# An adaLN-conditioned MoE FFN on one core: condition matrices by one gather and a round trip through DRAM, input loads queued ahead, TensorE started on zeros

## The reference, cut to what matters

```python
# x (32, 64, 512), itok (32,) in 1..198, cond weights (200, 64, 64); E=8 experts, H=512, I=352
w   = weights[itok]                                   # one 64x64 matrix for each batch entry
x1  = einsum('bct,bcd->bdt', x, w)                    # conditioned tokens, N = 2048 rows of 512
logits = einsum('nh,eh->ne', x1, Wr); gate = softmax(logits)
top2_val, top2_idx = top_k(gate, 2)                   # capacity 640 rows an expert, rank by cumsum
y   = sum over the chosen experts of gate * (silu(x1 @ Wg.T) * (x1 @ Wu.T)) @ Wd.T
out = x + y
```

## Time and profile before

| | |
|---|---|
| median of 3 runs | 308.54 us (308.44 to 308.93) |
| profiled execution, first to last instruction | 318.2 us |
| start of the expert phase's first transposes in it | 67.25 us |
| PE busy from 75 to 300 us | 224.93 of 225 us |
| mean granted TensorE clock | 0.963 |

### The profile page before, as it was taken

How to read it: one execution, slowest core, us unless ns; L and a number is a source line. 1 busy time by engine, 2 the same in 40 slices (tenths; PEclk the granted TensorE clock), 3 DMA queues, 4 the chain that set the end, 5 groups by cost and what they waited for, 6 DMA issues and landing times.

```text
span 318.2 us, 4646 instructions
## 1 busy us (share of the span) xinstructions
PE 286.5 (90%) x1620; PEld 250.0 (79%) x1621; DVE 134.1 (42%) x259; ACT 125.5 (39%) x212; POOL 138.2 (43%) x128
## 2 busy tenths in 40 slices
PE   2944989898999999999999999999999999999940
PEld 2623645568989999999999999999999999999930
DVE  2305689533434443454345444434544444523200
ACT  2102247612444444543435354445435444523220
POOL 5772007840045443374533334753735456463130
PEclk9985999789999999999999999999999999999995
DMA  6846119399979487866866866979679686474422
GB/s 157 277 157 216 63 47 384 129 319 345 407 188 204 103 226 131 181 174 165 169 141 140 157 121 150 230 157 211 178 168 179 145 195 95 71 116 59 59 35 33
DMA packets 24991, 53.16 MB, mean 167 GB/s; under 512 B 3344, under 2 KB 3344, under 8 KB 24976
## 3 DMA queue, kind: packets, MB, share of 16 engines
q0 software_dynamic: 9472, 21.67, 36.5%
q1 hardware_dynamic: 15504, 31.29, 30.2%
HBM read 32.69 MB, written 20.25 MB: 166 GB/s over the span
## 4 chain that ended last, share of the span: by engine, by line
PE 83%; DVE 4%; POOL 4%; another core or an unknown queue 3%; DMA 1%; issue 1%; ACT 1%; SPq 0%; ACTq 0%; DVEq 0%
PE bank L853 43%; PE bank L873 23%; PE bank L836 5%; PE bank L897 4%; POOL whi L397 3%; PE bank L736 3%; PE bank L825 2%; PE bank L748 1%; DMA x_sb<-x 1%; PE bank L771 1%; PE bank L758 1%; PE bank L780 1%; POOL out L422 0%; DVE tiles L595 0%
## 5 line engine op out<-in xcount | busy, mean ns | idle before, releaser
L422 POOL DMA_INDIRECT out<-tiles,dst_row x40 | 66.9, 1672 | 44.4 <-DMA out<-tiles,dst_row 21.2
L410 POOL DMA_INDIRECT tiles<-xf_dram,src_row x40 | 42.8, 1069 | 96.2 <-ACT tiles L504 66.3
L853 PE MATMUL bank<-whi,xhi 128*128 128x352 f32 x280 | 73.4, 343 | 0.8 <-ACT xhi L488 0.8
L853 PE MATMUL bank<-wlo,xhi 128*128 128x352 f32 x280 | 67.9, 323 | 0.0
L853 PE MATMUL bank<-whi,xlo 128*128 128x352 f32 x280 | 56.7, 324 | 0.0
L853 PEld LDWEIGHTS bank<-wlo,xhi 128*128 128x128 f32 x280 | 48.9, 188 | 0.0
L696 DVE TENSOR_TENSOR xlo<-bank,xhi 128x512 fp32r<-128x512 f32 x35 | 24.2, 692 | 56.5 <-ACT xhi L488 53.0
L853 PEld LDWEIGHTS bank<-whi,xlo 128*128 128x128 f32 x280 | 47.0, 189 | 0.0
L853 PEld LDWEIGHTS bank<-whi,xhi 128*128 128x128 f32 x280 | 45.7, 189 | 1.3 <-issue 1.3
L488 ACT ACTIVATE xhi<-bank 128x512 fp32r<-128x512 f32 x35 | 21.0, 599 | 61.7 <-PE bank L836 60.1
L873 PE MATMUL bank<-whi,hhi 128*128 128x512 f32 x105 | 41.4, 395 | 1.4 <-DVE hlo L720 1.4
(11 more groups left out here) (92 smaller groups left out, 256.3 us busy)
## 6 DMA issues: line engine op xcount, KB each, us to landing
raw<-wgu SPq DMA_DIRECT2D x32, 352.0 KB
x_sb<-x SPq DMA_DIRECT2D x8, 512.0 KB, 3.8
raw<-wd SPq DMA_DIRECT2D x8, 512.0 KB
out<-x_sb SPq DMA_DIRECT2D x4, 1024.0 KB, 8.3
xf_dram<-tiles SPq DMA_DIRECT2D x7, 520.0 KB, 4.0
raw<-wd SPq DMA_DIRECT2D x8, 192.0 KB
out<-x_sb SPq DMA_DIRECT2D x1, 1280.0 KB, 14.8
tiles<-xf_dram,src_row POOLq DMA_INDIRECT x40, 4.6
```

Of the source, the lines that this page charges most:

```text
L410: nc.gpsimd.indirect_dma_start(out=xg[:, n % TPE, :], out_offset=None, in_=xf_dram[:, :], in_offset=bass.IndirectOffsetOnAxis(ap=src_row[: ...
L422: nc.gpsimd.indirect_dma_start(out=out[:, :], in_=y_sb[:, n % TPE, :], in_offset=None, out_offset=bass.IndirectOffsetOnAxis(ap=dst_row[:, ...
L853: last = nc.tensor.matmul(ps[:, 0:I], left[:, b, c], right[:, half, o:o + I], start=(k == 0 and left is xhi and right is whi), stop=(k == ...
```

## The change

The 16 gathers, the index arithmetic (cidx), the copies into the block diagonal and their semaphores go. The indices come in by one load issued from ACT. One indirect DMA brings 32 whole condition matrices of 16 KB, one a partition, into wsel_sb, a part of the buffer raw that the expert weights use later. SP stores them to a DRAM buffer, waits until they are there, and issues two loads that write the two diagonal blocks of all tiles, straight into wbd. SP issues six x loads with no wait between them, then does that round trip, then issues the last two. The router weights come padded from the host, so the clear of wr_sb ahead of their load goes. PE starts with ten bf16 matmuls on a tile of zeros. Tile 15 is copied by ACT instead of DVE. logits(0) and logits(1) move ahead in PE's order, logits(2) and (3) stand together, and all six early condition matmuls stand behind them; gates is cut in two, and ACT's second exp moves behind three xf copies.

```diff
@@ sync
-            for half in range(2):
-                sp.dma_start(condb[half * C:(half + 1) * C, :],
-                             cond[half:half + 1, :].broadcast_to([C, TT])).then_inc(cond_in, 16)
             load_x(0)
-            sp.wait_ge(wr_clear, 1)
-            sp.dma_start(wr_sb[:, :, 0:E],
-                         wr.rearrange("(k p) e -> p k e", p=P)).then_inc(wr_in, 16)
-            for m in range(1, TT // 2):
-                if m >= 2:
-                    sp.wait_ge(x_in[m - 2], 16)
+            sp.dma_start(wr_sb[:, :, :], wr[:, :, :]).then_inc(wr_in, 16)
+            for m in range(1, X_FIRST):                      # X_FIRST = 6
+                load_x(m)
+            sp.wait_ge(wsel_in, 16)
+            sp.dma_start(wsel_dram[:, :], wsel_sb).then_inc(wsel_out, 16)
+            sp.wait_ge(wbd_clear, 1)
+            sp.wait_ge(wsel_out, 16)
+            wsel_t = wsel_dram.rearrange("(j t) (c d) -> t c j d", t=2, d=D)
+            for t in range(2):
+                sp.dma_start(wbd[t * C:(t + 1) * C, :, t * D:(t + 1) * D],
+                             wsel_t[t]).then_inc(wbd_in, 16)
+            for m in range(X_FIRST, TT // 2):
                 load_x(m)
-            sp.wait_ge(wc_in[NG - 1], 16 * GR)
@@ gpsimd
-            pool.wait_ge(cidx_ok, 1)
-            for j in range(TT):
-                nc.gpsimd.indirect_dma_start(
-                    out=wc_sb[:, j, :], out_offset=None, in_=wcond[:, :],
-                    in_offset=bass.IndirectOffsetOnAxis(ap=cidx[:, j:j + 1], axis=0),
-                ).then_inc(wc_in[j // GR], 16)
+            pool.wait_ge(cond_in, 16)
+            nc.gpsimd.indirect_dma_start(
+                out=wsel_sb, out_offset=None, in_=wcond[:, :],
+                in_offset=bass.IndirectOffsetOnAxis(ap=condb[:, 0:1].bitcast(U32), axis=0),
+            ).then_inc(wsel_in, 16)
@@ scalar
+            act.dma_start(condb[:, :], cond[:, :]).then_inc(cond_in, 16)
@@ tensor
+            pe.wait_ge(warm_clear, 1)
+            for _ in range(WARM_UP):                         # WARM_UP = 10
+                nc.tensor.matmul(ps_lg[0][:, :], warm[:, 0:P], warm[:, :], start=True, stop=True)
```

More of the change, by code:

```diff
@@ L39 @@
 BEFORE_RANKS = 6
+X_FIRST = 6
+WARM_UP = 10
 KEEP_WARM = 5
@@ L93, in build @@
         carry = sb("carry", [P, E, A])
-        condb = sb("condb", [P, TT], I32)
-        cidx = sb("cidx", [P, TT], U32)
-        wc_sb = sb("wc_sb", [P, TT, D])
+        condb = sb("condb", [B, 1], I32)
+        warm = sb("warm", [P, H], BF16)
         wbd = sb("wbd", [P, TT, 2 * D])
@@ L167, in build @@
         x_in = [sem(f"x_in{m}") for m in range(TT // 2)]
[L168 to L171, removed]
+        wsel_in = sem("wsel_in")
+        wsel_out = sem("wsel_out")
+        wbd_in = sem("wbd_in")
         tT_ps = sem("tT_ps")
-        tT_even_ok = sem("tT_even_ok")
-        tT_odd_ok = sem("tT_odd_ok")
+        tT_act_ok = sem("tT_act_ok")
+        tT_dve_ok = sem("tT_dve_ok")
         xrT_ps = sem("xrT_ps")
@@ L219, in build @@
         out_t = out[0:N, :].rearrange("(j p) h -> p j h", p=P)
+        TURN_ACT = [j for j in range(TT) if j % 2 == 0 or j == TT - 1]
+        TURN_DVE = [j for j in range(TT) if j not in TURN_ACT]
         def tile(i, s):
@@ L355, in _ @@
         def _(pool):
[L357 to L363, removed]
             nc.gpsimd.memset(ident[:, :], 0.0).then_inc(consts, 1)
-            pool.wait_ge(consts, 3)
+            pool.wait_ge(consts, 1)
             nc.gpsimd.affine_select(out=ident[:, :], in_=ident[:, :], compare_op=ALU.not_equal,
@@ L451, in xf_copy @@
                                      ACT.Copy).then_inc(xf_ok, 1)
-            for j in range(0, TT, 2):
+            act.dma_start(condb[:, :], cond[:, :]).then_inc(cond_in, 16)
+            for j in TURN_ACT:
                 act.wait_ge(tT_ps, j + 1)
@@ L457, in _ @@
                                      ps_tT[j % XR][:, :].rearrange("p (k c) -> p k c", k=KH),
-                                     ACT.Copy).then_inc(tT_even_ok, 1)
+                                     ACT.Copy).then_inc(tT_act_ok, 1)
             exps(0)
[L461 to L468, removed]
+            for n in range(XR - 1):
+                xf_copy(n, n)
             exps(1)
-            for n in range(1, XR):
-                xf_copy(n, n)
+            xf_copy(XR - 1, XR - 1)
             with act.Fori(1, TT // XR) as i:
@@ L530, in _ @@
         def _(dve):
[L531 to L548 removed]
+            nc.vector.memset(warm[:, :], 0.0).then_inc(warm_clear, 1)
+            nc.vector.memset(wbd[:, :, :], 0.0).then_inc(wbd_clear, 1)
+            nc.vector.memset(raw[IR:P, DOWN + (KI - 1) * H:WC], 0.0).then_inc(pad_ok, 1)
             chain = [0]
@@ L728, in _, with turned @@
         def _(pe):
+            def turned(j):
+                if j in TURN_ACT:
+                    pe.wait_ge(tT_act_ok, TURN_ACT.index(j) + 1)
+                else:
+                    pe.wait_ge(tT_dve_ok, TURN_DVE.index(j) + 1)
             def x_tile_turn(j):
@@ L740, in router @@
             def router(g):
-                pe.wait_ge(tT_even_ok, (g + 1) * (GR // 2))
-                pe.wait_ge(tT_odd_ok, (g + 1) * (GR // 2))
+                for j in range(g * GR, (g + 1) * GR):
+                    turned(j)
                 if g >= 1:
@@ L791, in _ @@
                     x_tile_turn((g + 1) * GR + 1)
+                else:
+                    logits(0)
                 router(g)
@@ L795, in _ @@
                     x_tile_turn((g + 1) * GR + 3)
-                if g == NG - 1:
-                    logits(0)
+                else:
+                    logits(1)
                 turn(g)
-            for g in range(1, NG):
+            for g in range(2, NG):
                 logits(g)
-                condition(g - 1)
-            for j in range(NG - 1, BEFORE_RANKS):
+            for j in range(BEFORE_RANKS):
                 condition(j)
```

67 lines of the change are left out of this document (29 added, 38 removed).

## The result

The change makes the kernel slower: 317.6 us, the median of four runs (315.35 to 319.96), against 308.5 for before on the same chip (308.31 to 308.93), ratio 1.030 (1.0273 to 1.0327). The forecast was slower, 312.9; the time lies 4.7 above it and 2.1 above the range. The execution profiled is the slowest of the four.

The account below looks back on a forecast made before the run. The expert phase is TensorE-bound and untouched, so time follows oh, set by the routing prologue's x loads: x_in6 at 20.2 + 7.4 + 10.1 = 37.7 against 33.3, 4.4 later, 308.5 + 4.4 = 312.9 us; range 304.0 to 315.5.

Parts of the forecast that it names:

- the cleaned timeline: Before's profile with two unexplained waits taken out: bound by x loads, router(3) ends at 23.3, oh at 33.3, span 306.2 us.
- the two pieces: Waits of 4.96 and 4.90 us without known releaser in before's profiled prologue, taken as absent from the timed executions.
- landed at 9 to 12, hidden: Gather takes 4.6 to 7 us, hidden under x loads; it and five x loads share 356 GB/s, 8.8 us, x_in5 at 13.1.
- 1.9 behind x load 5: Round trip's store, queued behind five x loads in SP's queue, lands 1.9 us after x_in5, at 15.0.
- The wbd loads and x load 6: Behind the store in SP's queue: wbd loads take 3.8 us, to 18.8; x_in6 follows 1.4 later, at 20.2.
- Pause and clock: PE pauses 5.6 us for x_in6, loses the high clock, regains it after 5; router(3) ends 7.4 after x_in6, at 27.6.
- 10.1, nothing: After router(3), logits, conditions, copy and second exp bring oh 10.1 us later, against 10.0 before: no change.
- A: The main forecast, oh at 37.7 and 312.9 us, own range 311 to 315; chance 0.48.
- B: Clock isn't lost, or loads come at their lower bound: oh at 33.5 to 35.3, 308.7 to 310.5 us; chance 0.15.
- C: Transfers are shorter without a profile: x_in6 at 17, clock kept, oh at 32.1, 307.3 us; chance 0.07.
- D: Both unexplained waits are in timed executions too, caused by the 16 gathers: oh 7.6 us earlier, 300.9 us; chance 0.17.
- E: Clock returns only after 8.5 us (transposes don't count as busy), 314.7, or 256-byte rows cost 1.5, 314.4; both 316; chance 0.13.

Follow-up runs that it names:

- a_same: The changed kernel itself, unchanged, on chip 11, timed beside before: 317.1 us against 308.2, ratio 1.029.
- a_4k: Changed kernel gathering 4 KB quarters into 128 partitions (4b + q), store writing 128 consecutive rows of 4 KB; chip 2: 312.6 us against before's 308.8, ratio 1.014.
- a_4k32: Changed kernel with four gathers of 4 KB quarters into the same 32 partitions, store unchanged; chip 2: 317.9 us against before's 308.8, ratio 1.029.
- a_gfirst: Changed kernel with x loads 1 to 5 issued only after the gather has landed; chip 6: 319.2 us against before's 320.7, ratio 0.994.
- a_best: a_4k with X_FIRST = 8, router(3) and turn(3) ahead of all logits, xr_sum(3) ahead of gates_first(0); chip 2: 311.5 us, ratio 1.011 to before.
- a_bestexp: a_best with exps(1) directly behind exps(0), ahead of the xf copies; chip 8: 309.8 us against before's 308.6, ratio 1.004.
- a_4knw: a_4k without the ten matmuls on zeros (WARM_UP = 0); chip 2: 312.5 us against before's 308.6, ratio 1.012.
- b_free: Before with only its hold on the x loads taken away, the 16 gathers kept; chip 6: 320.5 us against before's 320.7, ratio 1.000.
- b_same: Before itself, unchanged, one profiled execution on chip 11: 308.1 us, before there 308.2.
- a_x8: Changed kernel with all eight x loads ahead of the store (X_FIRST = 8); chip 6: 318.9 us against before's 320.7, ratio 0.995.
- a_nowarm: Changed kernel without the ten matmuls on zeros (WARM_UP = 0); chip 6: 316.4 us against before's 320.7, ratio 0.986.

## Why the prediction was wrong, step by step

**What bounds it, and the cleaned timeline: right.** The undisturbed before has span 306.3 (306.2 forecast) and oh at 33.4 (33.3). That the two pieces weren't in the timed runs was right in every comparison but that on chip 6, where before took 319.7 to 321.6 in seven runs, with spans of 318.0 to 319.9. The first profile's span of 318.2 fits these and not the timed runs beside which it was set.

**The gather, "landed at 9 to 12, hidden": this step failed, and with it the term 6 x 1.47 = 8.8 for five x loads and the gather.** The gather landed at 15.9 (14.4 in a_same), and from the landing of x load 0 to that of x load 5 it took 14.5 us (13.2 in a_same): x load 5 came at 19.1 instead of 13.1. I priced the gather by bytes, from the 4.6 us of a gather with 128 partitions, and let it share the x loads' 356 GB/s. Filling 32 partitions it moved less for the same engine time, and so did everything beside it: the transposes of tiles 10 and 11 began at 20.4 instead of ending by 15.

a_4k changed the layout of gather and store (and, with it, how the indices are made), and its timeline is near the forecast's: x loads 0 to 5 in 8.2 us (8.8), gather landed 11.4 (9 to 12), store landed 14.8 (15.0), transposes of tiles 10 and 11 done at 15.3 (15), x load 6 at 21.6 (20.2), router(3) done at 29.5 (27.6), oh 39.5 (37.7). Its time of 312.6 against the forecast's 312.9 is closer than its parts, by luck: oh came 1.8 us later than forecast, and from oh to the end it takes 271.1 us where before takes 272.9. Some 0.8 of this gain lies ahead of the expert phase's first gate/up matmuls, where the clock was at 0.50 for a shorter time; the rest I haven't placed. By time 4.5 us of the 9.1 are this step (a_same 317.1, a_4k 312.6), by oh 4.1.

The Trainium skill ("SBUF — State Buffer", Door 1: The DMA port swizzle) says that partitions 0 to 31 reach 8 of the 16 DMA ports of the memory. An estimate from it: with half the ports a 4 KB piece would take up to twice its 164 ns, 328. It took 260 in a_4k32, and 339 (a quarter of 1357) in the whole rows, so the gathers agree in direction. The store of a_gfirst doesn't: 611 ns for 16 KB are 153 for 4 KB, out of the same 32 partitions. The forecast lacked this rule. That the ports are the mechanism is not shown; that the layout is the cause is, for the gather and what runs beside it.

**The store, "1.9 behind x load 5": right in kind, too long by some 0.6.** It landed 1.2 to 1.3 us behind the last x load ahead of it in ten of the kernels with 32 or 128 rows (in the changed kernel 20.3 behind 19.1, in a_4k 14.8 behind 13.5), 1.9 in a_4k32. Its 4.4 us from its own issue in the changed kernel hold a wait for x load 5. But the late gather would have been enough: its landing at 15.9 plus the 3.3 us of a_4k's store are 19.2.

**The wbd loads and x load 6.** 5.2 us from the first issue of the two to x load 6's landing was forecast (15.0 to 20.2); it was 20.4 to 27.0, 6.6, and 6.7 in a_4k. The term was 1.4 short. It lies in the pair, 5.4 us from its first issue to its last landing where 3.8 was forecast; x load 6 followed 1.2 behind (1.4). The 256-byte pieces took 18 ns each, 2048 of them on 16 engines: 2.3 us where 524 KB at 356 GB/s are 1.5.

**Pause and clock: right.** 5.1 us of pause (5.6), the clock at 0.50 behind it, 7.3 us from x load 6 to router(3) (7.4; 7.9 in a_4k). The clock also fell at about 11 us, after the first waits for x loads, which the forecast didn't have. The ten matmuls on zeros took 3.7 us, where the forecast had 4.3.

**From router(3) to oh, "10.1, nothing": right in a_same (10.0), short in the profiled execution**, 11.7, where the clock fell once more at 38 us and the second exp, behind three copies, waited for conditions at 1.2 GHz. That order costs nothing in a_same, but is what a_best then hits: removing it (a_bestexp) gave 1.6 to 1.7 us.

**Rivals.** A was the shape, with the round trip as the price, but its sum was 4.7 short, and the gather's step above is worth 4.1 to 4.5 of that. B and C didn't come. D's condition holds on chip 6 alone, and there three variants of the changed kernel are 0.5 to 1.4% faster than before, and have no such pieces. Its gain of 7.6 us didn't come even there (1.5 to 4.3), since the late gather still costs what it costs. E didn't come: the clock was back 4 to 5 us after x load 6 in the changed kernel, about 5.5 in a_4k. And the rule of the Trainium skill that the prediction names under E isn't borne out by the two lines of a_4knw above, where it rose behind 24 transposes and nothing else.

**Still open:** what causes the pieces of 5 us on chip 6 (three kernels with one gather hadn't them, b_free had; that the 16 gathers are the cause was not tried there). The x loads' data wasn't late: their packets are all there, the last over by 20.4 us in the first profile of before and by 17.1 in b_free (19.9 in b_same). But of the 16 semaphore records of a landing these two traces hold few (for x load 7 none and two), where b_same has all 16; that marks the disturbed profiles and doesn't explain them. Open as well: why the same store takes 611 ns a piece or twice that, and why GpSimd's queue lets its two loads wait so long beside weight loads.

## What to carry to other kernels

Price a DMA by where it lands as well as by its bytes: count the partitions it fills and look at the first dimension on each side, and compare GB/s at equal DMA share before calling a transfer hidden. A round trip through memory in one in-order queue is paid by everything queued behind it; moving the load ahead only hands the wait to the round trip, and each wait removed here uncovered the next (block diagonal, matmul order, exp, ranks), until five edits (layout, X_FIRST, TensorE's order, VectorE's sum, the exp) came within 0.4% of the kernel that paced its loads. Time the kernel before on each chip anew: on one it was 4% slower, with two waits that no variant of the changed kernel had.

## What the hardware showed that I had not expected

- 32 partitions instead of 128: a 4 KB piece of an indirect gather 260 ns instead of 164, one of 16 KB 1059 alone and 1357 to 1437 beside x loads, and the whole traffic with it 230 instead of 392 GB/s at a DMA share of 1.03 in both.
- The store out of these 32 partitions: 611 ns for 16 KB in a_gfirst and a_x8, 1087 to 1262 in a_same, a_nowarm, a_4k32 and the changed kernel.
- The store queued behind x loads landed 1.2 to 1.3 us behind the last of them in ten kernels, with 32 rows of 16 KB or 128 of 4 KB.
- 24 fp32 transposes and nothing else, from 5.4 us on, and the router behind them ran at the higher clock (a_4knw).
- A store whose destination has a first dimension of 4: 8.5 us for 128 pieces of 159 ns; with 128 rows 1.9.
- Two loads of 256-byte pieces by GpSimd's queue with weight loads beside them: 10.2 us, by SP's 4.7.
- Before at 308.2 to 308.8 us on three numbered chips and 320.7 on a fourth (b_free's profile there: two waits of 4.2 and 5.0 us with no releaser, which are 9 of the 12).
